# Eight transformer layers on one core: q turned by VectorE and DRAM, two heads per column group, ternary tails in one product

## The chip, the cores and the metric

The program runs on one NeuronCore of a Trainium2 chip. The metric is the device time of one execution in microseconds (us). A core has TensorE (matrix products and transposes through its array, PE in the profile), VectorE (DVE), ScalarE (ACT), GpSimd (POOL), SyncE (SP, which here only issues DMAs) and 16 DMA engines. Each engine runs its own instruction list in order and meets the others at semaphores. TensorE writes to PSUM, which the kernel uses as eight banks of 128 partitions x 512 float32 columns.

## The reference, cut to what matters

The input x is 16 tiles of 128 rows x 256 columns; the context has 128 rows x 128 columns per tile. Eight layers follow each other, each of the form x = x + layer(layernorm(x)): attention and feed-forward in turn. Three attention layers and one feed-forward are touched:

```python
# first attention: 32 heads of 8, rotary positions on q and k
logits = jnp.einsum('bqhd,bkhd->bhqk', rope(x @ Wq), rope(k)) / sqrt(8)
out = einsum('bhqk,bkhd->bqhd', softmax(logits), v) @ Wout + bout    # one softmax per head
# small-head attention (third attention): 16 heads of 16, q and k normalised per head
#   two softmaxes per head: over the 112 main keys and over the last 16 keys
ctx = attn(q, k, v) + attn(q, k_dca, v_dca);  out = ctx @ Wo + bo
# ternary feed-forward: 682 hidden columns
h1 = x @ tern(w1).T; h3 = x @ tern(w3).T;  out = (silu(h1) * h3) @ tern(w2).T
# wide attention (fourth attention): 16 heads of 128
q = rmsnorm(x @ Wq, gq); k = rmsnorm(ctx @ Wk, gk)
out = (softmax(q @ k.T / sqrt(128)) @ v) @ Wo
```

(The excerpt is condensed; the shapes are those of the reference.) The other layers are a product-key feed-forward, a grouped attention with 16 heads of 128, a routed mixture of experts and a feed-forward with block-quantised operands.

## The kernel before, in words

The work is cut into stages 0 to 7, one for each layer (the mixture of experts has the sub-stages 3, 8 and 9), and each stage into steps. A step is done for each tile b and, in some, for parts c. `STEPS` lists for each stage its steps, their parts and the engines that have a share in them (T, V, A, G, S for TensorE, VectorE, ScalarE, GpSimd, SyncE); `ONCE` lists work done once per stage. `ORDER` holds one long string for each engine: each letter is the next part of one step, so the order of every engine's whole program is written out, and stages overlap where the strings mix them. `BANKS` gives the PSUM banks of each step; a helper `room` makes TensorE wait until the bank's last content was taken, `full` and `freed` give the semaphore and count at which a bank has been filled or emptied. A wait stands ahead of the instruction that needs it, and everything behind it on that engine waits too.

**Stage 0** (`small_heads` with s = 0). Per tile: layer norm (`lnA`, `lnB`), transposes of the normalised tile (`xT`), q and k in one bank (`qk`, L943 to L948), rotation (`rope`, L1821 to L1823 on VectorE, L2520 on GpSimd), a split of q and k into float16 high parts and rests (`split`: ScalarE L1433, GpSimd's two copies L2525 and L2526, VectorE's two subtractions L1867 and L1868, all at once), 16 float16 transposes (`tqk`, L971), score products for the row maximum (`mx`, L995), eight maxima (`mxr`, L1887), transposes of q with its maximum (`tq2`, L1024), score products again with keys in rows (`st`, L995), eight exponentials (`ex`, L1465), and value products (`pv`, L1042): for each part c four products of one head each, 32 output partitions by 128 columns. Eight parts fill two banks, `oa` and `ob`, that is 1024 columns, of which 9 rows in 32 are used (8 values and the sum of the exponentials). Two copies (`ot`, L1472), eight transposes back (`tb`, L1052), two divisions (`norm`, L1907 and L1911), the output product (`oT`, `out`).

**Stage 4** (`small_heads` with s = 4) is alike with 16 heads of 16. Its two kinds of score products are interleaved: a step `ms` (L1016 and L1012) holds maximum products of tile b in one pair of banks (3 and 4) and softmax products of tile b - 1 in another (5 and 6); `sl` does the last tile's. Four matmuls in turn use four groups of 32 array rows. k's scale and bias are applied by VectorE while it copies the transposes (L1878, L1879); v is copied by VectorE in two masked forms with its bias (`vp`, L1899). The inverse roots of 32 variances per row are GpSimd's (`nb`, L2533).

**Stage 5** (`ternary`). w1 and w3 as signs in bfloat16; the 682 hidden columns are five tiles of 128 and one of 42 for each of w1 and w3. Step `h` (L1274) with c = 1 does the last full tile and the 42-column tile of each, six products per tile of columns (three bfloat16 parts of x, two halves of the inner dimension).

**Stage 6** (`wide_heads`). 16 tiles x 4 parts = 64 steps, four heads of 128 in each. q (L1301, L1302) goes to bank 0; ScalarE copies it (L1644) and squares it (L1647); TensorE transposes it head by head (`tq`, L1314) and ScalarE copies the transposes with a scale (L1658). k (L1308) is squared (L1652), normalised (L2313 on VectorE, L2564 and L2566 on GpSimd, L2324), turned in blocks of 32x32 by VectorE (L2333), written to DRAM by a DMA from GpSimd's queue (L2555) and read back by four DMAs from SyncE's queue (L866), which completes the 128x128 transpose. Score products (L1323), row maximum (L2347), exponentials with their sums (L1673), the reciprocal and the multiplication of P (`pn`, L2356 and L2358 on VectorE), P's own turn (L2341, L2560, L866), the product with the context (`pv`, L1329), a copy (L1664) and the output product (`wo`, L1337).

**Stage 7** (`quantized`) runs in part beside stage 6: products L1359, L1360 and L1376; on VectorE a chain of operations over 1024 columns (L2368 to L2391).

## Time and profile before

| | us |
|---|---|
| timed runs | 2088.37, 2077.08, 2078.17 |
| median | 2078.17 |
| profiled execution | 2088.02 |
| its span | 2085.8 |
| mean granted TensorE clock | 0.989 of full |
| busy: TensorE / VectorE / ScalarE / GpSimd | 1997.6 / 1713.2 / 1274.0 / 667.7 |

The span runs from the first to the last instruction. Busy time is the union of the instructions of an engine; waiting, semaphores and the issuing of DMAs are not in it, save that GpSimd's DMA instructions count as its own. A matmul's end is modelled, so a group of pipelined matmuls looks some 0.2 us longer than the time until the next group may start. One float32 matmul of the program appears as two MATMUL rows (a transpose as one).

### The profile page before, as it was taken

What the parts mean: (1) busy time and instruction counts of PE and PEld (TensorE: products, weight loads), DVE (VectorE), ACT (ScalarE), POOL (GpSimd) and SP (SyncE); (2) the same over time, 40 slices, a digit from 0 to 9 for tenths busy, and PEclk for the clock granted to TensorE, in tenths of its full rate; (3) what the DMA queues carried; (4) which work ended last, traced back from release to release, by engine and by line L of the source; (5) the groups of instructions that cost most, each with busy time, mean ns of one, the idle gap of its engine ahead of it and who ended that gap; (6) DMA issues with size and microseconds to landing.
All of it is one profiled execution on the core that took longest, in us unless ns stands there. A gap on an engine that the chain in (4) does not pass through costs nothing.

```text
span 2085.8 us, 46042 instructions
## 1 busy us (share of the span) xinstructions
PE 1997.6 (96%) x16294; PEld 1564.6 (75%) x16294; DVE 1713.2 (82%) x4655; ACT 1274.0 (61%) x3214; POOL 667.7 (32%) x1000
## 2 busy tenths in 40 slices
PE   5999899999999999998998889999999999999998
PEld 3666799999988888877997667887665666656665
DVE  7887899999689997766447789896887998888877
ACT  3778988798944554544653444634766666567552
POOL 6321020000012232222128776111665345434420
PEclk8999999999999999999999899999999999999999
DMA  9400300000045443433220010023544233333320
GB/s 336 144 3 2 124 6 2 2 2 2 12 151 168 137 151 104 142 102 89 89 65 26 29 62 2 2 87 122 166 150 133 91 112 114 127 105 107 122 81 25
DMA packets 181515, 182.28 MB, mean 87 GB/s; under 512 B 20678, under 2 KB 160088, under 8 KB 180264
## 3 DMA queue, kind: packets, MB, share of 16 engines
q1 hardware_dynamic: 160168, 112.49, 17.5%
q0 software_dynamic: 21120, 66.87, 8.8%
q8 instruction: 130, 2.13, 0.4%
q14 instruction: 97, 0.79, 0.1%
HBM read 99.06 MB, written 80.22 MB: 86 GB/s over the span
## 4 chain that ended last, share of the span: by engine, by line
PE 53%; DVE 29%; issue 7%; ACT 4%; POOL 4%; DMA 3%; SPq 1%; another core or an unknown queue 0%; DVEq 0%; ACTq 0%; POOLq 0%
PE pb L1141 4%; PE pb L1164 3%; PE pb L1274 3%; PE pb L1337 2%; PE pb L1042 2%; PE pb L1149 2%; PE pb L1376 2%; PE pb L1359 2%; PE pb L1222 2%; PE pb L1360 2%; PE pb L1156 2%; PE pb L1283 2%; PE pb L995 2%; PE pb L1213 2%; PE pb L1329 1%
## 5 line engine op out<-in xcount | busy, mean ns | idle before, releaser
L2472 POOL TENSOR_SCALAR sm<-sm 128x1 f32<-128x1 f32 x128 | 33.7, 263 | 455.9 <-DVE sm L1745 454.9
L1508 ACT ACTIVATE areaB<-i128h,workB 128x128 f16<-128x128 f16 x512 | 156.2, 392 | 0.1
L1465 ACT ACTIVATE areaA<-pb 128x512 f32<-128x512 f32 x192 | 106.8, 600 | 61.6 <-PE pb L1012 35.2
L1535 ACT ACTIVATE workA<-workA 128x128 f32<-128x128 f32 x256 | 99.4, 390 | 60.8 <-DVE workA L2059 55.5
L1673 ACT ACTIVATE workA<-pb,workA 128x128 f32<-128x128 f32 x256 | 113.9, 460 | 30.9 <-DVE workA L2351 30.3
L1097 PE MATMUL pb<-areaB 128*128 128x128 f32 x1024 | 126.7, 280 | 3.1 <-ACT workB L1498 2.9
L1141 PE MATMUL pb<-xT,areaA 128*128 128x128 f32 x1024 | 124.2, 276 | 0.0
L1097 PEld LDWEIGHTS pb<-areaB 128*128 128x128 f32 x1024 | 119.8, 194 | 5.6 <-ACT workB L1498 3.3
L1141 PEld LDWEIGHTS pb<-xT,areaA 128*128 128x128 f32 x1024 | 120.0, 192 | 4.5 <-issue 4.0
L1164 PE MATMUL pb<-areaA,workA 128*128 128x256 f32 x512 | 121.6, 382 | 0.9 <-ACT workA L1542 0.9
L1337 PE MATMUL pb<-areaA,workA 128*128 128x256 f32 x512 | 120.7, 380 | 0.0
L2541 POOL DMA_DIRECT2D turn<-workA x64 | 37.1, 580 | 245.3 <-DVE workA L2072 244.8
L1113 PE MATMUL pb<-areaB,workB 128*128 128x256 f32 x512 | 113.7, 380 | 1.1 <-DVE workB L2036 1.1
L1337 PEld LDWEIGHTS pb<-areaA,workA 128*128 128x128 f32 x512 | 95.0, 190 | 25.3 <-issue 12.9
L1164 PEld LDWEIGHTS pb<-areaA,workA 128*128 128x128 f32 x512 | 93.8, 190 | 21.6 <-issue 8.5
L1113 PEld LDWEIGHTS pb<-areaB,workB 128*128 128x128 f32 x512 | 96.0, 190 | 13.9 <-DVE workB L2036 1.3
L1887 DVE TENSOR_REDUCE workA<-pb 128x4 f16<-128x512 f32 x128 | 83.4, 689 | 13.9 <-PE pb L995 13.5
L1042 PE MATMUL pb<-areaA,workA 128*32 128x128 f32 (+1 forms) x1536 | 86.4, 285 | 5.3 <-ACT areaA L1465 4.3
L2533 POOL TENSOR_TENSOR areaA<-areaA,neghalf 128x32 f32<-128x32 f32 x16 | 87.6, 5475 | 1.3
L1323 PEld LDWEIGHTS pb<-workA 128*128 128x128 f32 x512 | 65.1, 191 | 21.7 <-issue 18.6
L2474 POOL TENSOR_TENSOR sm<-sm,neghalf 128x1 f32<-128x1 f32 x128 | 76.7, 599 | 10.7
L1664 ACT COPY workA<-pb 128x512 f32<-128x512 f32 x64 | 37.8, 590 | 66.5 <-PE pb L1329 66.0
(426 smaller groups left out, 5872.0 us busy)
## 6 DMA issues: line engine op xcount, KB each, us to landing
turn<-workA POOLq DMA_DIRECT2D x64, 256.0 KB
workA<-turn SPq DMA_DIRECT2D x256, 64.0 KB
turn3k<-areaA POOLq DMA_DIRECT2D x64, 256.0 KB, 2.7
workA<-turn3k SPq DMA_DIRECT2D x256, 64.0 KB, 2.0
turn3p<-areaA POOLq DMA_DIRECT2D x64, 256.0 KB, 2.7
rows_in<-areaB SPq DMA_DIRECT2D x7, 2048.0 KB, 16.5
areaA<-turn3p SPq DMA_DIRECT2D x168, 64.0 KB, 2.0
workA<-turn3p SPq DMA_DIRECT2D x88, 64.0 KB, 2.0
```

What stands on the lines that cost most here:

```text
L1042: m = eng.matmul(p[r, k * 128:(k + 1) * 128], vt[:, h, :], P[:, j * 128:(j + 1) * 128], start=True, stop=True)
L1097: m = eng.matmul(p[:, e * 128:(e + 1) * 128], w.ed[:, k, (4 * c + e) * 128:(4 * c + e + 1) * 128], xT[:, k, :], start=(k == 0), stop=(k == 1))
L1113: m = eng.matmul(p[:, 0:256], G[:, e, :], w.eu[:, e, :], start=(e == 0), stop=(e == 15))
L1141: m = eng.matmul(p[:, h * 128:(h + 1) * 128], w.wq[:, 4 * c + h, k], xT[:, k, :], start=(k == 0), stop=(k == 1))
L1164: m = eng.matmul(p[:, 0:256], u.OT[i][:, h], w.wo[:, 4 * c + h], start=(c == 0 and h == 0), stop=(c == 3 and h == 3))
L1337: m = eng.matmul(p[:, 0:256], u.OT[i][:, h], w.wo[:, 4 * c + h], start=(c == 0 and h == 0), stop=(c == 3 and h == 3))
L1465: eng.activation(u.P[n % RP], bank(*held)[:, :], ACT.Exp, scale=1.0 / math.sqrt(hd)).then_inc(freed(*held)[0], 1)
L1508: m = eng.activation(u.far[:, g], i128h[:, :], ACT.Square, bias=u.at[b % 2][:, 8 * c + g:8 * c + g + 1])
L1535: m = eng.activation(u.P[i][:, h], u.P[i][:, h], ACT.Exp, accum_out=u.den[i][:, h:h + 1], bias=u.nm[i][:, h:h + 1])
L1673: m = eng.activation(u.P[i][:, h], p[:, h * 128:(h + 1) * 128], ACT.Exp, accum_out=u.den[i][:, h:h + 1], bias=u.nb[i][:, h:h + 1], scale=u ...
L1887: eng.tensor_reduce(o[:, :, 24:25], p, AX.X, ALU.max, negate=True).then_inc(freed(s, tag, b, c // 2)[0], 1)
L2533: eng.tensor_tensor(va, va, neghalf[:, 0:32], ALU.pow).then_inc(S["l2_rs"], 1)
```

## The change

What it does:

- Stage 6: VectorE turns q out of PSUM in blocks of 32x32, GpSimd's queue writes it to DRAM (`turn3q`), SyncE's queue reads it back in four DMAs, ScalarE scales it from SBUF into the place that the scores product reads. TensorE's step `tq` and ScalarE's plain copy of q are gone. q's products use banks 0 and 3 in turn. The multiplication of P by the reciprocal moves from VectorE to GpSimd.
- Stage 0: the second half of the heads is laid 16 columns later in its 32-column group of the value operand, so that heads of parts c and c + 4 accumulate in one group of 32 partitions; one bank `o` of 512 columns replaces `oa` and `ob`; one copy, four transposes, one division. The rows of Wout are permuted on the way in. The two subtractions of the split move from VectorE to GpSimd, behind its copies.
- Stage 4: `mx` and `st` are separate steps of 16 matmuls over four row groups; both use the banks 3 to 6. k's scale and bias and v's two masked forms move from VectorE to ScalarE; v's bias is added at the output transposes' copy (two ScalarE passes in place of one copy).
- Stage 5: the 42 last columns of w1 and the 42 of w3 (rolled to the front of their block) stand 64 columns apart and are done by one product of 106 columns.
- Stage 3: TensorE's rank product waits for the position of the tile before (`m_pos`).
- The strings of `ORDER` are new for all engines.

```diff
# TensorE, stage 0: value products, back transposes
-                    k = (c - c0) * (E // 32) + E * j // 128
+                    k = c % 4 if s == 0 else (c - c0) * 2 + j // 2
                     m = eng.matmul(p[r, k * 128:(k + 1) * 128], vt[:, h, :], P[:, j * 128:(j + 1) * 128],
-                                       start=True, stop=True)
+                                       start=(s == 4 or c == 0), stop=(s == 4 or c == 7))
+                elif step == "tb" and s == 0:
+                    t.wait_ge(*freed(0, "o", b))
+                    p = room(0, "r", b)
+                    for k in range(4):
+                        m = eng.transpose(p[:, k * 128:(k + 1) * 128], u.OTs[b % 2][:, k * 128:(k + 1) * 128], ident)
...
# GpSimd, stage 0: split
                     eng.tensor_copy(qp[:, 0, :, 16:24], qp[:, 0, :, 0:8])
                     eng.tensor_copy(qp[:, 1, :, 8:16], qp[:, 1, :, 0:8])
+                    eng.tensor_tensor(qp[:, 0, :, 8:16], y4[:, 0], qp[:, 0, :, 0:8], ALU.subtract)
+                    eng.tensor_tensor(qp[:, 1, :, 16:24], y4[:, 1], qp[:, 1, :, 0:8], ALU.subtract).then_inc(S["l0_split"], 1)
...
# stages 0 and 4: score products (a step of stage 4 is now all four row groups)
+                    rows = range(2 * (c % 2), 2 * (c % 2) + 2) if s == 0 else range(4)
+                    tags = [step + "ab"[i % 2] if s == 0 else f"{step}{i}" for i in rows]
+                    p = [room(s, tag, b, c) for tag in tags]
-    (4, "ms"): lambda b, c: (("mxa", 3), ("mxb", 4)) + ((("sta", 5), ("stb", 6)) if b else ()),
+    (4, "mx"): lambda b, c: (("mx0", 3), ("mx1", 4), ("mx2", 5), ("mx3", 6)),
+    (4, "st"): lambda b, c: (("st0", 3), ("st1", 4), ("st2", 5), ("st3", 6)),
...
# ScalarE, stage 4: k's scale and bias, v's two forms
+                            eng.activation(dst[:, :, 0:112], src[:, :, 0:112], ACT.Identity, scale=w4.nwc[:, 1:2], bias=w4.nwc[:, 4:5])
+                            eng.activation(dst[:, :, 112:128], src[:, :, 112:128], ACT.Identity, scale=w4.nwc[:, 2:3],
+                                           bias=w4.nwc[:, 5:6]).then_inc(freed(4, "tk", b)[0], 1)
+                    for k in range(2):
+                        m = eng.activation(u.vt[b % RV][:, :, 17 * k:17 * k + 16], src, ACT.Copy, scale=side[k])
...
# TensorE, stage 3
+                    if b > 0:
+                        t.wait_ge(S["m_pos"], b)
...
# TensorE, stage 5
+                        tiles = [(128 * m_, at + 128 * (4 * c + m_), 128) for m_ in range(4 if c == 0 else 1)]
+                        if c == 1 and tag == "h3":
+                            tiles.append((128, 640, 106))
...
# stage 6: TensorE, VectorE, GpSimd, SyncE, ScalarE
-    (6, "q"): lambda b, c: (("q", 0),),
+    (6, "q"): lambda b, c: (("q", (0, 3)[c % 2]),),
-                elif step == "tq":
-                    t.wait_ge(S["l3_qn"], nth(b, c, 4))
-                    p = room(6, "tq", b, c)
-                    for h in range(4):
-                        m = eng.transpose(p[:, h * 128:(h + 1) * 128], u.qn[i][:, h * 128:(h + 1) * 128], ident)
+                    eng.transpose(u.Dq[n % 2].rearrange("p (j h w) -> p j h w", j=4, h=4),
+                                  bank(6, "q", b, c)[:, :].rearrange("p (h j w) -> p j h w", h=4, j=4)).then_inc(S["l3_qt"], 1)
+                    eng.dma_start(turn3q[n % 4], u6.Dq[n % 2].rearrange("p (j w) -> p j w", j=4)).then_inc(S[f"l3_qw{n % 2}"], 16)
+                    turned_in(turn3q[n % 4], u6.qr[n % 2], S[f"l3_qr{n % 4}"])
+                    eng.activation(u.qT[i].rearrange("p h (i w) -> p h i w", i=4),
+                                   u.qr[i].rearrange("p (i h w) -> p h i w", i=4, h=4), ACT.Copy, scale=gp[:, 0:1]).then_inc(S["l3_qg"], 1)
-                    eng.tensor_tensor(u.P[i], u.P[i], bc(u.rec[i], 2, [128, 4, 128]), ALU.mult).then_inc(S["l3_pn"], 1)
+                elif step == "pn":
+                    g.wait_ge(S["l3_rec"], nth(b, c, 4))
+                    P, rec = u6.P[c % 2], u6.rec[c % 2]
+                    eng.tensor_tensor(P, P, bc(rec, 2, [128, 4, 128]), ALU.mult).then_inc(S["l3_pn"], 1)
```

## Rows read from the trace of the kernel before

**Rows 1.** The page, busy time of each engine and the chain that ended last.

```profile
PE 1997.6 (96%) x16294; PEld 1564.6 (75%) x16294; DVE 1713.2 (82%) x4655; ACT 1274.0 (61%) x3214; POOL 667.7 (32%) x1000
...
PE 53%; DVE 29%; issue 7%; ACT 4%; POOL 4%; DMA 3%; SPq 1%; another core or an unknown queue 0%; DVEq 0%; ACTq 0%; POOLq 0%
```

**Rows 2.** Windows: from:to, length, busy PE, PEld, DVE, ACT, POOL (count), clock, DMA, GB/s.

```profile
50.00:200.00 150.00, 147.51 (x2418) 101.86 (x2411) 127.13 (x272) 116.94 (x218) 36.92 (x69) 1.00 0.17 56
...
1110.00:1310.00 200.00, 175.55 (x1963) 138.41 (x1961) 166.11 (x463) 88.67 (x163) 145.75 (x121) 0.94 0.09 28
...
1450.00:1600.00 150.00, 145.45 (x633) 93.63 (x634) 120.37 (x258) 107.61 (x291) 89.69 (x147) 1.00 0.50 160
...
1450.00:2086.00 636.00, 617.62 (x2542) 397.61 (x2542) 531.32 (x1008) 389.53 (x975) 271.26 (x436) 1.00 0.35 113
```

**Rows 3.** TensorE by shape: busy us, mean ns, idle; last: duration min/median/max, first, last.

```profile
L1314 PE MATMUL pb<-cst,workA 128*128 128x128 f32 x256 | 38.5, 273 | 1.5 <-ACT workA L1658 1.0 <-ACT xT L1422 0.4
...
L1274 PE MATMUL pb<-workB,areaB 128*128 128x128 bf16 x960 | 60.4, 219 | 0.0
...
L1274 PE MATMUL pb<-workB,areaB 128*42 128x128 bf16 x192 | 16.4, 221 | 0.0
...
L1191 PE MATMUL pb<-workB,cst x16: 166/169/180, 626.2 to 959.7; 128*128 128x8 f16 x16
```

**Rows 4.** TensorE in order of time: start us, us, line.

```profile
118.75 0.61 PE L1052 MATMUL pb<-cst,areaA 128*128 128x128 f32 x4
...
119.28 0.40 PE L995 MATMUL pb<-workA 32*128 32x128 f16 x8
...
1710.11 0.60 PE L1314 MATMUL pb<-cst,workA 128*128 128x128 f32 x4
...
1710.55 1.02 PE L1329 MATMUL pb<-areaA,workA 128*128 128x512 f32 x2
```

**Rows 5.** VectorE, groups by shape.

```profile
L2333 DVE STREAM_TRANSPOSE areaA<-workA 128x512 f32<-128x512 f32 x64 | 45.1, 704 | 11.5 <-DMA turn3k<-areaA 9.1 <-ACT areaA L1637 1.9
...
L2358 DVE TENSOR_TENSOR workA<-workA 128x512 f32<-128x512 f32 x64 | 44.5, 696 | 2.2
...
L1889 DVE TENSOR_REDUCE workA<-pb 128x4 f32<-128x448 f32 x64 | 39.5, 617 | 10.2 <-PE pb L1016 6.3 <-remote 3.8
...
L1899 DVE SCALAR_TENSOR_TENSOR workA<-pb,cst,areaA 128x256 f32<-128x256 f32 x32 | 13.9, 475 | 0.2 <-PE pb L962 0.2
...
L1878 DVE TENSOR_SCALAR workA<-pb,areaA 128x448 f32<-128x448 f32 x16 | 11.8, 737 | 2.6 <-PE pb L979 2.6
...
L1879 DVE TENSOR_SCALAR workA<-pb,areaA 128x64 f32<-128x64 f32 x16 | 5.3, 334 | 0.0
```

**Rows 6.** ScalarE, groups by shape.

```profile
L1465 ACT ACTIVATE areaA<-pb 128x512 f32<-128x512 f32 x192 | 106.8, 600 | 61.6 <-PE pb L1012 35.2
...
L1658 ACT ACTIVATE workA<-pb,gp 128x512 f32<-128x512 f32 x64 | 44.6, 696 | 22.1 <-PE pb L1314 22.1
```

**Rows 7.** GpSimd, groups by shape.

```profile
L2515 POOL TENSOR_TENSOR x<-x,areaA 128x256 f32<-128x256 f32 x32 | 24.0, 758 | 15.1 <-DVE xn L1755 15.1
...
L2520 POOL TENSOR_TENSOR workA<-workA 128x512 f32<-128x512 f32 x16 | 20.6, 1286 | 9.0 <-DVE workA L1868 5.4 <-DVE workA L1823 3.7
```

**Rows 8.** Lines L1867 and L2566: duration ns min/median/max.

```profile
L1867 DVE TENSOR_TENSOR workA<-workA x16: 415/421/1484, 23.3 to 189.9; 128x256 f16<-128x256 f32 x16
...
L2566 POOL TENSOR_TENSOR workA<-workA,neghalf x64: 1006/1032/2027, 1431.7 to 1997.8; 128x4 f32<-128x4 f32 x64
```

**Rows 9.** DMA: issue on GpSimd, KB and us to landing, SyncE's issue of four.

```profile
L2555 POOL DMA_DIRECT2D turn3k<-areaA x64 | 38.7, 605 | 56.4 <-DVE areaA L2333 55.6 <-issue 0.4
...
turn3k<-areaA POOLq DMA_DIRECT2D x64, 256.0 KB, 2.7
...
areaA<-turn3p SPq DMA_DIRECT2D x168, 64.0 KB, 2.0
...
1699.85 1.77 SPq L866 DMA_DIRECT2D areaA<-turn3p  x4
```

More of the change, by code:

```diff
@@ L557, in program @@
         w4.mu = carve(32)
-        w4.bvs = [carve(256).rearrange("p (h e) -> p h e", e=16) for _ in range(2)]
+        w4.bvT = carve(4).rearrange("p (j k) -> p j k", j=2)
+        w4.bsum = carve(2)
         carve = carver(area[0], 4096)
@@ L609, in program @@
         u6.kn = carve(512)
-        u6.qn = [carve(512) for _ in range(2)]
+        u6.Dq = [carve(512) for _ in range(2)]
         u6.qT = [carve(512).rearrange("p (h n) -> p h n", n=128) for _ in range(2)]
+        u6.qr = [work[1][:, 8704 + 512 * k:9216 + 512 * k] for k in range(2)]
         u6.kT = [carve(512) for _ in range(2)]
@@ L980, in small_heads @@
                         m.then_inc(full(s, tag, b)[0], 1)
-                elif step in ("mx", "st") and s == 0:
+                elif step in ("mx", "st"):
                     if step == "mx":
@@ L1444, in small_heads @@
                     if b >= RQ and step == "tqk":
-                        a.wait_ge(*full(*scores(s, 1, b - RQ, ng // 2 - 1)))
+                        a.wait_ge(*full(*last_square(s, "st", b - RQ)))
                     if s == 0:
@@ L1476, in small_heads @@
                         a.wait_ge(*full(s, "out", b - 2))
-                    eng.copy(u.OT[b % 2], bank(s, "oT", b)[:, 0:256].rearrange("p (k n) -> p k n", k=2)
-                             ).then_inc(freed(s, "oT", b)[0], 1)
+                    src = bank(s, "oT", b)[:, 0:256].rearrange("p (k n) -> p k n", k=2)
+                    if s == 0:
+                        eng.copy(u.OT[b % 2], src).then_inc(freed(s, "oT", b)[0], 1)
+                    else:
+                        for k in range(2):
+                            m = eng.activation(u.OT[b % 2][:, k], src[:, k], ACT.Identity, bias=w4.bsum[:, k:k + 1])
+                        m.then_inc(freed(s, "oT", b)[0], 1)
             def peer(step, b, c):
```

395 lines of the change are left out of this document (197 added, 198 removed), and 23 rows, old and new, of tables (ONCE, STEPS, TAKEN).

## The prediction

> **What bounds the kernel now.** I read the busy shares first, then the chain of waits, the windows by stage, and the groups by shape of the engines that the change touches. TensorE is busy 96% of the span and carries 53% of the chain that ended last; VectorE, the second, is busy 82% and carries 29% [rows 1]. The windows show where each bound sits [rows 2]. In the first attention (50 to 200 us) TensorE is busy 147.5 of 150 us. Where the fifth layer's small-head attention runs (1110 to 1310 us) it is busy 175.6 of 200: there 24.4 us are idle, VectorE is busy 166.1, and the granted clock of 0.94 shows that part of the stretch ran at 1.2 GHz instead of 2.4. In the wide attention and the last feed-forward (1450 to 2086 us) TensorE is busy 617.6 of 636, VectorE 531.3, ScalarE 389.5, GpSimd 271.3. So an instruction taken off TensorE shortens stage 0 and stages 6 and 7 nearly at its price, if nothing comes late in its place; in stage 4 VectorE and the order of hand-overs decide as well.
>
> A group's busy time is too dear a price for a matmul, since it holds the pipelined tail of the last one. The timeline gives the rate [rows 4]: four transposes are shown as 0.60 us, but the next product starts 1710.55 - 1710.11 = 0.44 us after the first of them. In the first attention the same four occupy 119.28 - 118.75 = 0.53 us.
>
> **The change, part by part.**
>
> Wide attention (stage 6, 64 steps). Four TensorE transposes go from every step: 64 x 0.44 = 28.2 us off the engine; the group's 38.5 us is the upper bound [rows 3, 4]. Their work moves:
> - VectorE turns q out of PSUM. The same shape from SBUF takes 704 ns [rows 5], so 45.1 us come. Nothing shows this turn with a PSUM source; The ends I keep are 0.60, the shortest ScalarE pass over 512 columns [rows 6], and 0.84 us, VectorE's PSUM read of 448 columns in 737 ns scaled to 512 [rows 5]; I take the SBUF row, as the same operation. In return the multiplication of P leaves VectorE: 64 x 696 ns = 44.5 us. VectorE stays at about 531 us, against 636 - 28 = 608 us of stage: 87%.
> - ScalarE drops the plain copy of q (about the 0.60 us of a 512-column pass [rows 6]) and keeps the scaling copy of 696 ns [rows 6], now from SBUF. It is busy 390 of 636 us, so this gives nothing.
> - GpSimd gets the multiplication and one more DMA issue. Its nearest row is the 128x512 addition, 1286 ns [rows 7]; the issue of an equal block is 605 ns [rows 9]. So 64 x 1.89 = 121 us come, and GpSimd stands at 271 + 121 = 392 of 608 us. But the opening of the stage is denser: in 1450 to 1600 it is busy 89.7 us with 19 steps [rows 2], and 19 x 1.89 = 36 makes 126 of 150. The next LayerNorm statistics, both reciprocal roots and three DMA issues queue behind each multiplication.
> - SyncE issues four more reads per step, 1.77 us for four [rows 9]: with q it issues three sets, 5.3 us, in a step of 608 / 64 = 9.5 us.
> - q's road to the scores product is now 0.70 (turn) + 0.61 (issue) + 2.7 (landing) + 1.77 + 2.0 (four reads, landing) + 0.70 (scaling) = 8.5 us, where it was a copy, four transposes and a copy, 1.8 us. In the new order of TensorE's queue I counted the work that stands between the q product and the scores product of the same step, at 0.43 us for 512 columns: 8.0 us at the least, 14.8 in the median. Without queueing on the way one step is short, by 0.5 us; with 1 us of queueing six are, by 5.9 us together; with 3.5 us eleven, by 25. k's road is longer still, but k is issued earlier (median 25 us). The P road grows by 1.29 - 0.70 = 0.6 us, and the order gives it 20 us in the median where it gave 17. I take 6 us of new idle time in all; the ends are 0 and 64 x 1.3 = 83 us (the rival below).
> Net: 28.2 - 6 = 22 us.
>
> First attention (stage 0, 16 tiles). Two heads now share 32 output partitions, so the output is 512 columns and not 1024; the number of value products is the same. Four of the eight back transposes go: 16 x 0.53 = 8.6 us; upper bound 16 x 0.61 = 9.8 us [rows 4]. ScalarE loses one copy and VectorE one division of 16 heads per tile: both hidden. The two subtractions of the split move from VectorE to GpSimd: 2 x 758 ns by the 128x256 addition [rows 7], 24 us in a stage where GpSimd is busy 36.9 of 150 us. They were done beside the copies on GpSimd and now come after them, so TensorE's transposes of q and k start about 1 us later in each tile's chain; the next tile's work covers it, and without that cover it costs 16 us. I take 8.6 us.
>
> Ternary layer (stage 5). The two products of 42 columns per part become one of 106: 12 instructions to 6 per tile, 96 in all. The streamed operand is 128 columns either way. At the main form's 60.4 / 960 = 63 ns this is 6.0 us; at the narrow form's 16.4 / 192 = 85 ns, 8.2 [rows 3]. I take 6.
>
> Small-head attention (stage 4). The score products of max and softmax no longer run interleaved in two pairs of banks; both now use the same four banks, in turn. Their number and their rotation over four row groups stay. VectorE sheds k's scaling (737 + 334 ns) and v's two masked forms (2 x 475): 2.0 us per tile, 32 us in all, to ScalarE, which was busy 88.7 of the 200 us [rows 2, 5]; the bias of the output, now two passes instead of one copy, is ScalarE's too. That lets TensorE come nearer to its own work; all 24.4 us of idle time is the most it can give. Against it stands the hand-over of banks. After the max products four pairs of reductions must run, 4 x 617 ns and four over the other 64 columns at 334 ns or less, 2.5 to 3.8 us [rows 5], and after the softmax products four exponentials, 2.4 us [rows 6], before the other kind may start. The new order puts 1.3 to 5 us of other TensorE work between them; adding up where it is less than needed I get some 10 us of sure idle time, in place of the stalls that were there. I take a gain of 4 us, between +24 and -20.
>
> The new wait of the rank product on the previous tile's position costs nothing: the 16 rank products are spread over 626 to 960 us [rows 3], some 20 us apart, and only the few small VectorE operations of one tile stand between rank and position.
>
> **Sum.** 22 + 8.6 + 6 + 4 = 41 us. The profiled execution took 2088.0 us (span 2085.8), so it would take 2047. The three timed runs have a median of 2078.2, 9.9 below the profiled one; with the same saving the median comes to 2037 us.
>
> **A rule weighed.** Rows first [rows 8]: VectorE's subtraction with two SBUF operands takes 421 ns in the median and 1484 at worst, and GpSimd's power of four elements 1032 and 2027. So the two engines do hold each other up, by about one instruction of the other.
> The Trainium skill (SBUF — State Buffer, Who interferes with whom) says that VectorE and GpSimd share one pair of SBUF ports under an exclusive lock, and that whoever comes second waits for the whole instruction. It speaks against moving a 128x512 multiplication to GpSimd. [...] The excess of 1.06 us in the rows agrees with a wait for one instruction.
>
> **Rivals.**
> 1. GpSimd's multiplication holds VectorE. Worked from rows: if each of the 64 blocked VectorE for its full 1.29 us, VectorE would have 531 + 82 = 613 us and bind the stage, which then saves nothing: gain 8.6 + 6 + 4 = 19, time 2060. For it: the worst cases above. Against it: most VectorE work there reads PSUM or one operand, and one such multiplication leaves VectorE itself.
> 2. The bank turn of stage 4 costs more: its idle time grows by 20 instead of shrinking by 4: 2078 - 41 + 24 = 2061. For it: the short gaps in the new order, each needing a prompt VectorE, and VectorE busy 83% there. Against it: its 32 us less of work.
> 3. Slower: q's road through DRAM sets the pace. GpSimd takes its turns in order, and in the opening of stage 6 it is at 84% or more; if q comes late by 1.3 us in each step, 83 us are lost and the 6 counted are not: 2078 - 41 - 6 + 83 = 2114. It decides from 41 / 64 = 0.64 us of mean lateness per step beyond what I counted. Against it: 14.8 us of cover in the median for a road of 8.5.
> 4. Better: TensorE keeps every instruction's group price and stage 4's idle time goes: 38.5 + 9.8 + 8.2 + 24.4 = 81, time 1997.
> That the work is not removed can be excluded: the transposes are gone from the program.
>
> **How the numbers follow.** Forecast 0.6, rivals 0.08, 0.12, 0.09, 0.11. The likeliest case itself spans 2022 to 2052 (new idle time in stage 6 of 0 to 15 us, stage 4 between +10 and -5). To leave out no more than 2 in 10 the range takes in rivals 1 and 2 and half of the way to 4: 2012 to 2066. What a measurement of this kernel can tell from no change is about 0.5%, 10 us: faster means under 2067.8, slower over 2088.6. Faster gets the forecast, rival 4 and two thirds of 1 and 2, 0.84, less 0.02 for what I did not see; same 0.08; slower 0.10 (rival 3 and a little).
>
> **What would show it.** Right: no transposes from the q step; TensorE busy about 40 us less and its share still 94% or more; the wide stretch about 22 us shorter; in it few waits of the scores product on ScalarE's scaled q; a turn of q near 0.70 us on VectorE and a multiplication near 1.29 on GpSimd; idle time of TensorE in the small-head stretch about 20 us. Wrong: TensorE waiting for the scaled q or for the reads of q in most steps (rival 3); VectorE over 95% there with lengthened instructions (1); first score products of stage 4 waiting for reductions or exponentials with more than 30 us in sum (2).

## The result and the profile after

The changed kernel takes 2076.02 us (median of 20 runs, 2072.09 to 2083.57); the kernel before took 2080.51 beside it (20 runs, 2075.52 to 2088.37). The ratio is 0.9979, 95% interval 0.9970 to 0.9987: 4.5 us faster. The interval leaves out 1, so the kernel is a little faster, but by less than half of the 0.5% that the prediction took as the least that can be told, and far from the 2037 us that were forecast. The profiled execution took 2075.69 us, span 2073.7.

The page after, answering to [rows 1]: 416 TensorE instructions and 44 us of its busy time are gone, and the span is 12 us shorter, not 40 (and 7 of the 12 were a lateness of that one execution of before, as shown below). Its share falls to 94%. In the chain that ended last, TensorE falls from 53% to 40%, and SyncE's queue, the DMAs and GpSimd rise from 8 to 16%.

```profile
PE 1953.9 (94%) x15878; PEld 1517.6 (73%) x15878; DVE 1683.4 (81%) x4527; ACT 1261.0 (61%) x3209; POOL 782.4 (38%) x1160
...
PE 40%; DVE 33%; issue 8%; POOL 7%; DMA 5%; SPq 4%; ACT 4%; DVEq 0%; POOLq 0%; ACTq 0%
```

The windows, with the columns of [rows 2]. In the opening of the wide attention TensorE was idle 4.6 of 150 us before and is idle 9.4 after, GpSimd is busy 118 us and not 90, and the DMA share is 0.73 instead of 0.50.

```profile
50.00:200.00 150.00, 144.55 (x2393) 97.76 (x2390) 114.31 (x222) 112.47 (x207) 49.32 (x95) 1.00 0.17 55
...
1450.00:1600.00 150.00, 140.60 (x543) 87.45 (x543) 125.91 (x264) 96.44 (x274) 118.34 (x185) 0.98 0.73 226
1450.00:2074.00 624.00, 583.37 (x2222) 362.23 (x2221) 525.56 (x981) 351.42 (x891) 351.02 (x538) 0.99 0.51 161
```

The new operations cost about what was estimated. These are the groups of the changed kernel for VectorE's turn of q, GpSimd's multiplication, its third issue and ScalarE's scaling, answering to [rows 5, 6, 7, 9]: 698 ns against 704 taken, 1067 against 1286, 592 against 605, and 726 against 696. On the right of each row stands how long the engine was idle before these instructions and what ended it: ScalarE stood 68.5 us for the reads of q (`turn3q`).

```profile
L2326 DVE STREAM_TRANSPOSE workA<-pb 128x512 f32<-128x512 f32 x64 | 44.6, 698 | 6.0 <-PE pb L1313 5.2 <-DMA turn3q<-workA 0.7
...
L2587 POOL TENSOR_TENSOR workA<-workA 128x512 f32<-128x512 f32 x64 | 68.3, 1067 | 19.6 <-DVE workA L2373 18.9
...
L2573 POOL DMA_DIRECT2D turn3q<-workA x64 | 37.9, 592 | 62.1 <-DVE workA L2326 61.6
...
L1688 ACT ACTIVATE workA<-workB,gp 128x512 f32<-128x512 f32 x64 | 46.5, 726 | 69.0 <-DMA workB<-turn3q 68.5 <-PE pb L1328 0.4
```

The waits of TensorE and of its weight loads in stages 6 and 7 (engine, line, what it waited for: us in total, times, longest). L1334 is the product with P, L1328 the scores. L1334 stood 30.7 us for turn3p in sum, L1328 17.6 us for ScalarE's scaled q.

```profile
PEld pb L1334 <- DMA areaA<-turn3p: 12.9, 11, 2.7
PEld pb L1328 <- ACT workA L1688: 12.0, 12, 2.1
PEld pb L1334 <- DMA workA<-turn3p: 7.6, 8, 2.9
...
PE pb L1328 <- ACT workA L1688: 5.6, 6, 1.3
PE pb L1334 <- DMA areaA<-turn3p: 5.5, 9, 1.8
PE pb L1334 <- DMA workA<-turn3p: 4.7, 3, 2.6
```

The same waits of the kernel before, whose product with P is L1329: 8.2 us.

```profile
PEld pb L1329 <- DMA workA<-turn3p: 3.5, 5, 1.0
...
PEld pb L1329 <- DMA areaA<-turn3p: 1.9, 3, 0.7
...
PE pb L1329 <- DMA workA<-turn3p: 1.6, 3, 0.8
PE pb L1329 <- DMA areaA<-turn3p: 1.2, 3, 0.5
```

### The profile page after: what moved, and what is told of

The parts are those of the page before. It is cut to its first block, busy times and chain, and to the rows that moved or that the text cites. A ratio compares the mean times of both kernels' runs of the same rounds, so it can differ in the third digit from the quotient of the medians.

```text
span 2073.7 us, 45659 instructions
## 1 busy us (share of the span) xinstructions
PE 1953.9 (94%) x15878; PEld 1517.6 (73%) x15878; DVE 1683.4 (81%) x4527; ACT 1261.0 (61%) x3209; POOL 782.4 (38%) x1160
## 4 chain that ended last, share of the span: by engine, by line
PE 40%; DVE 33%; issue 8%; POOL 7%; DMA 5%; SPq 4%; ACT 4%; DVEq 0%; POOLq 0%; ACTq 0%
PE pb L1148 3%; PE pb L1171 3%; SPq L877 3%; PE pb L1040 3%; PE pb L1013 3%; PE pb L1156 2%; PE pb L1231 2%; PE pb L1163 2%; PE pb L1222 2%; DVE workB L1952 1%; PE pb L1120 1%; DVE workB L2042 1%; PE pb L1104 1%; POOL workA L2593 1%; DVE workB L2033 1%
## 5 line engine op out<-in xcount | busy, mean ns | idle before, releaser
L1104 PE MATMUL pb<-areaB 128*128 128x128 f32 x1024 | 124.6, 278 | 0.0
L1013 PE MATMUL pb<-workA 32*128 32x128 f16 (+2 forms) x2048 | 82.0, 252 | 9.7 <-DVE workA L1904 4.4
L1328 PEld LDWEIGHTS pb<-workA 128*128 128x128 f32 x512 | 65.2, 192 | 33.6 <-issue 20.9
L1688 ACT ACTIVATE workA<-workB,gp 128x512 f32<-128x512 f32 x64 | 46.5, 726 | 69.0 <-DMA workB<-turn3q 68.5
L1013 PEld LDWEIGHTS pb<-workA 32*128 32x128 f16 (+2 forms) x2048 | 58.9, 140 | 39.2 <-issue 24.9
```

The lines of the kernel that those rows point to most:

```text
L1013: m = eng.matmul(p[k][:, j * 128:(j + 1) * 128], one, two, start=True, stop=True)
L1104: m = eng.matmul(p[:, e * 128:(e + 1) * 128], w.ed[:, k, (4 * c + e) * 128:(4 * c + e + 1) * 128], xT[:, k, :], start=(k == 0), stop=(k == 1))
```

## The experiments

Whole runs of this kernel scatter by some 5 us, and chips differ: the median of before was 2080.5 to 2087.5. So the ratio is given, and beside it a measure that scatters less, called the stretch from here on: from the first q product of stage 6 to the last output product of stage 7, by the first and last starts of those lines. For the changed kernel it is 2070.7 - 1426.4 = 644.3 us:

```profile
L1312 PE MATMUL pb<-areaA,xT x128: 592/592/1061, 1426.4 to 1994.7; 128*128 128x512 f32 x128
```

```profile
L1381 PE MATMUL pb<-areaB,workB x256: 379/379/455, 1617.2 to 2070.7; 128*128 128x256 f32 x128
```

A second trace of the changed kernel gives 644.4. The kernel before was traced again too, since its first trace came from an execution of 2088.0 us, 7.5 over its median:

> The kernel before, unchanged, for a second trace of it: the first came from an execution of 2088.0 us where its median was 2080.5. If the 8 us lie in its stages 0 to 5, the last product of stage 5 stands here at about 1430 us instead of 1439, and stages 6 and 7 (first q to last output product) at 636 us in both. If they lie in stages 6 and 7, that stretch is here near 629 us, and then the changed kernel's 644 is 15 us longer, not 8.

This execution took 2081.15 us; the stretch is 2076.0 - 1440.3 = 635.7, and it was 636.0 in the first trace. So the 7 us lay ahead of stage 6 (first q at 1440.3 here, 1446.9 there).

```profile
L1301 PE MATMUL pb<-areaA,xT x128: 592/592/697, 1440.3 to 1992.2; 128*128 128x512 f32 x128
```

```profile
L1376 PE MATMUL pb<-areaB,workB x256: 379/379/454, 1631.0 to 2076.0; 128*128 128x256 f32 x128
```

The wide attention and what follows it thus became 8.5 us longer, where 22 us shorter was forecast: 30 us are missing. The windows over the stretch, with the columns of [rows 2], for the kernel before (second trace), the changed kernel, and the changed kernel without any road for q (e4 below):

```profile
1440.30:2076.00 635.70, 619.61 (x2552) 399.52 (x2551) 531.09 (x1007) 391.15 (x978) 271.47 (x436) 1.00 0.36 115
...
1426.40:2070.70 644.30, 603.13 (x2301) 373.93 (x2300) 538.15 (x1003) 365.45 (x917) 364.58 (x562) 0.99 0.52 165
...
1432.30:2048.20 615.90, 593.91 (x2300) 373.13 (x2300) 500.77 (x939) 393.02 (x981) 327.88 (x498) 1.00 0.36 118
```

TensorE is idle 16.1 us before and 41.2 us after: 25 us of new idle time, where 6 were taken. And its busy time falls by 16.5 us, not by the 25.7 of e4, though it does the same products: in three stretches of 20 us (from 1446, 1506 and 1906 us) the changed kernel was granted a clock of 0.91, and some products took up to 1061 ns where the median is 592.

The table has all runs of these two stages, with what each does in a few words. A ratio has 1.8 to 6 us of uncertainty. The stretch stands on one trace for each run, save where two are given. Traces of one kernel differ by 0.1 to 0.3 us in it, but e9 and e11, which differ only in the bytes of a write whose data nobody uses, by 4.4. Differences of a few us between two rows are to be read with that in mind.

| kernel | stages 6 and 7, us | ratio to before [95%] |
|---|---|---|
| before | 636.0, 635.7 | 1 |
| changed | 644.3, 644.4 | 0.9979 [0.9970, 0.9987], again 0.9984 [0.9974, 0.9994] |
| e1: P divided on VectorE | 650.1 | 0.9989 [0.9973, 1.0006] |
| e3: both parts undone | 637.0, 636.7 | 0.9955 [0.9937, 0.9973], 0.9950 [0.9930, 0.9970] |
| e2: old order, division alone on GpSimd | 712.1 | 1.0301 [1.0273, 1.0329] |
| e12: the same, placed otherwise | 706.7 | 1.0280 [1.0267, 1.0294] |
| e4: q without any road | 615.9 | 0.9838 [0.9813, 0.9864] |
| e5: + VectorE's turn | 624.3 | 0.9884 [0.9864, 0.9904] |
| e9: + GpSimd's write | 632.3 | 0.9935 [0.9915, 0.9955] |
| e11: e9 with a small write | 636.7 | 0.9930 [0.9915, 0.9944] |
| e10: + four small reads | 635.4 | 0.9932 [0.9911, 0.9954] |
| e6: + reads in full | 643.8 | 0.9968 [0.9953, 0.9983] |
| e7: changed, ScalarE off q's road | 642.3 | 0.9967 [0.9954, 0.9980] |
| e8: changed, one read for four | 641.4 | 0.9958 [0.9944, 0.9971] |
| e16: changed, q's write by SyncE | 674.2 | 1.0127 [1.0099, 1.0155] |

**Each part undone.**

```
- eng.reciprocal(u.rec[i], u.den[i]).then_inc(S["l3_rec"], 1)      # e1; GpSimd's "pn" empty
+ eng.reciprocal(u.rec[i], u.den[i]).then_inc(*v.mark()); v.settle()
+ eng.tensor_tensor(u.P[i], u.P[i], bc(u.rec[i], ...), ALU.mult).then_inc(S["l3_pn"], 1)
```

> The changed kernel, but the division of P in the wide attention is VectorE's again (reciprocal, then the multiplication straight behind it); q still goes through DRAM. In the changed kernel a step's P reaches its turn 4.4 us after the reciprocal ends, before 1.45 us. Theory A (P's road is late, because GpSimd takes its instructions in order and P's multiplication stands behind other work and waits there): most of the 36 us that stages 6 and 7 lost comes back, 2050 to 2058 us, and the waits of the pv product on turn3p fall from 31 us of idle time to under 12. Theory B (q's own road makes the scores late: ScalarE waits 68 us in all for q's reads and the score products 18 us for ScalarE): little changes, 2070 to 2078, and the score waits stay. Theory D (SyncE's queue and the DMA traffic of twelve issues a step delay every road alike): 2066 to 2076, waits for both stay at half or more. VectorE as the bound (64 x 0.7 = 45 us more work on it) would give 2080 or more.

Nothing comes back: the stretch gets 6 us longer, the ratio moves by 0.001, which its interval can't tell from none. By the timeline's means over 64 steps, P's way from the end of the reciprocal to the start of its turn is 4.4 us in the changed kernel (1.45 before) and 4.5 in e1: the new order has the turn later anyway. So e1 does not shorten P's road and can't clear it; it shows that in this order the division on GpSimd costs nothing, and by the stretch of one trace gains 6 us.

e3 takes the code and the queue orders of the kernel before for stages 6 and 7 and leaves the rest changed.

> Stages 6 and 7 wholly as in the kernel before (q transposed on TensorE, P divided on VectorE, the old order), stages 0 to 5 as changed. The trace has the last product of stage 5 26.5 us earlier and the first q of stage 6 20.5 us earlier than before, and stages 6 and 7 took 639 us before against 648 us after. If the parts add up, 2080.5 less 20 to 26 = 2054 to 2060 us. If the gain of the stages ahead is swallowed at the boundary (the weights of stage 6 or 7 arrive late, or the clock falls), 2066 to 2076.

> The run with both parts of the wide attention undone, timed again beside the changed kernel on one chip. It was at 0.9955 of the kernel before, with stages 6 and 7 at 637 us (before 636, changed 644). Expected 0.993 to 0.997, and 3 to 8 us below the changed kernel.

> The changed kernel, unchanged, on the same chip as the run with both parts undone: 0.997 to 0.999 of the kernel before; stages 6 and 7 again near 644 us.

The marks of the second run of e3, 2071.9 - 1435.2 = 636.7:

```profile
L1470 PE MATMUL pb<-areaA,xT x128: 592/592/697, 1435.2 to 1987.5; 128*128 128x512 f32 x128
```

```profile
L1545 PE MATMUL pb<-areaB,workB x256: 379/379/454, 1627.5 to 2071.9; 128*128 128x256 f32 x128
```

The stretch is as before, to 1 us. Timed beside each other on one chip, e3 ran in 2076.7 us (median of 7), the changed kernel in 2083.2 (11), the kernel before in 2087.1: the change to stages 0 to 5 alone is the best version that leaves nothing out, 10.4 us under before. (20 to 26 were expected in the first run; they came from the first trace of before, with its 7 us of lateness.) So the wide attention's edit costs 6.5 us by the times and 7.5 by the stretch.

**The division alone.** e2 has e3's code and orders, with P's multiplication moved to GpSimd and VectorE's turn of P one instruction later; e12 has the turn further back and GpSimd's order taken from VectorE's.

> Stages 6 and 7 in the order and with the q transposes on TensorE of the kernel before; of the change to the wide attention only the division of P on GpSimd is kept, with VectorE's turn of P one instruction later in its order. All other stages as changed. Starting point is 2080.5 - 24.5 (what the changed stages 0 to 5 gained in the trace) = 2056. Theory A (the multiplication on GpSimd costs lateness whatever q does): 2066 to 2080. Theory B or D (it is q's road that costs): 2050 to 2058.

> Stages 0 to 5 as changed; in stages 6 and 7 q is transposed on TensorE in the order of the kernel before, and the division of P is on GpSimd as in the run that came to 1.030, but placed otherwise: VectorE's turn of P stands three instructions behind the reciprocal, not one, and GpSimd takes its instructions in the order in which VectorE releases them. If that run's 64 us came from VectorE standing at its turn for the product (69 us of idle time there), this one is at 0.990 to 1.000, and if the division on GpSimd frees VectorE to some use, below the run with both undone (0.9955). If it came from the longer road of P itself, it stays above 1.010.

By the stretch they are 75 and 70 us slower than e3; e12 lies where a longer road of P was to put it. In e2 VectorE stood at its turn for the product:

```profile
DVE areaA L2523 <- POOL workA L2749: 71.7, 41, 3.2
```

In e12 that is mostly gone (12.7 us), but now the product with P waits on TensorE. The rows of its weight loads and its matmuls:

```profile
PEld pb L1503 <- DMA areaA<-turn3p: 29.3, 15, 6.0
PEld pb L1503 <- DMA workA<-turn3p: 14.7, 7, 7.8
```

```profile
PE pb L1503 <- DMA areaA<-turn3p: 24.4, 12, 5.2
PE pb L1503 <- DMA workA<-turn3p: 12.6, 5, 7.6
```

I read this as: the old order of TensorE has no room for a later P, the changed kernel's has. The same division on GpSimd costs 70 us in one order and nothing, or less than nothing, in another. (The two orders differ in more than P's place, so how much a still better placing would save stays open.)

**What q's road costs, piece by piece.** e4 lets ScalarE copy q and nothing else happen to it:

> The changed kernel with the transposition of q left out altogether: ScalarE copies q from the bank and scales the copy, nothing goes to VectorE, GpSimd or DRAM for it (the scores are those of an untransposed q). It shows what TensorE's 64 x 0.44 us are worth when q has no road. Theory A (P's road on GpSimd holds): no better than the changed kernel less a little, 2062 to 2074, pv still waits for turn3p. Theory B or D (q's road, or the traffic that it adds): 2036 to 2050, near the 2037 forecast. In between: both.

The gain is there: 615.9 us, 28.4 less than the changed kernel and 21 less than e3.

```profile
L1308 PE MATMUL pb<-areaA,xT x128: 592/592/697, 1432.3 to 1971.2; 128*128 128x512 f32 x128
```

```profile
L1377 PE MATMUL pb<-areaB,workB x256: 379/379/454, 1614.2 to 2048.2; 128*128 128x256 f32 x128
```

Theory A falls with it: GpSimd divides here as well, and P is nearly as late (4.2 us from reciprocal to turn, against 4.4). But the 21 us are not the transposes alone: without the division and without q's turn VectorE has 30 us less to do than before (500.8 against 531.1). With q's turn in, VectorE's work is back at 537.1 and 12.5 us of the gain over e3 are left (e5). Then the pieces of the road were put back one at a time.

```
  eng.activation(u.qT[i]...,                                      # e5, e6, e9 to e11: what ScalarE scales
-     u.qr[i]..., ACT.Copy, scale=gp[:, 0:1])                     #   what came back from DRAM
+     u.cx[:, 0:4]..., ACT.Copy, scale=gp[:, 0:1])                #   a resident block of the same size
- a.wait_ge(S[f"l3_qr{n % 4}"], 64 * (n // 4 + 1))
+ a.wait_ge(S["l3_qt"], n + 1)
  # e5: no write, no reads.  e9: write.  e11: write of rows 0 to 15.  e10: write, reads of 4 rows.  e6: all
```

> The changed kernel with VectorE's turn of q left in place, but no write to DRAM and no reads for q: ScalarE waits for the turn and then scales a resident block of the same size instead of the q that came back (q's values are left out of the scores). Against the kernel before, the changed kernel is at 0.998 and q with no road at all (no turn, no DMA) at 0.984. If VectorE's 64 turns of 0.70 us are what costs (VectorE is the engine busiest beside TensorE), this run is near 0.996 to 1.000. If it is the road through DRAM or its DMAs, it stays near 0.984 to 0.987.

```profile
L1308 PE MATMUL pb<-areaA,xT x128: 592/592/697, 1431.4 to 1977.2; 128*128 128x512 f32 x128
```

```profile
L1377 PE MATMUL pb<-areaB,workB x256: 379/379/454, 1614.8 to 2055.7; 128*128 128x256 f32 x128
```

> As the run with the turn alone, and now with the write to DRAM and the four reads of each step issued as in the changed kernel, but no computing engine waits for them: only SyncE, GpSimd and the DMA queues carry them (q's values are again left out of the scores). If the queues and the traffic are the cost (SyncE with twelve reads a step, GpSimd with three writes a step, DMA share 0.52 for 0.35, which delays K's and P's reads too), this run is at 0.994 to 0.999. If the cost is the latency of q's own road, for which ScalarE waits in its order (68 us of idle time there), it stays near the run with the turn alone, within 0.003 of it.

```profile
L1312 PE MATMUL pb<-areaA,xT x128: 592/592/1061, 1427.3 to 1993.4; 128*128 128x512 f32 x128
```

```profile
L1381 PE MATMUL pb<-areaB,workB x256: 379/379/454, 1619.2 to 2071.1; 128*128 128x256 f32 x128
```

> As the run with VectorE's turn alone (0.988 of the kernel before), plus GpSimd's issue of q's write and the write itself (64 x 0.59 us on GpSimd, 16.8 MB); SyncE reads nothing back. The same with the reads and no one waiting was 0.997. If GpSimd's third issue a step delays the writes of K and P, this run is at 0.994 to 0.997. If it is SyncE's four further reads a step or their bytes, it stays at 0.988 to 0.991.

```profile
L1308 PE MATMUL pb<-areaA,xT x128: 592/592/697, 1424.1 to 1979.5; 128*128 128x512 f32 x128
```

```profile
L1377 PE MATMUL pb<-areaB,workB x256: 379/379/454, 1609.5 to 2056.4; 128*128 128x256 f32 x128
```

> As the run with the write alone (0.9935; its stages 6 and 7 took 632 us in the trace, against 624 with the turn alone), but the write carries 16 of 128 rows, 32 KB for 256 KB; GpSimd issues it as often. If GpSimd's issuing in its order is the cost (64 x 0.59 us between its pow and multiplication instructions), stages 6 and 7 stay at 631 to 634 us and the ratio at 0.992 to 0.995. If it is the bytes of the write, 624 to 627 us and 0.988 to 0.990.

> As the run with all of q's DMAs and no one waiting (0.997), but each of the four reads of a step brings 4 rows x 4 pieces instead of 32 x 4, so 8 KB instead of 64 KB: SyncE issues as often, the queues carry an eighth. If the issuing on SyncE is what delays the reads of K and P, it stays at 0.994 to 0.998. If it is the bytes in the DMA engines, it falls to the time of the write alone, 0.988 to 0.992.

The pieces by the stretch:

- The turn on VectorE 8.4 us. Its ratio of 0.9884 lies between the two expectations, nearer to the second: it is a third of the loss, not all and not nothing. It is a net price, since ScalarE's plain copy of q goes in the same step.
- The write 8.0, and with an eighth of its bytes not less (636.7). So it is GpSimd's issue and not the bytes; VectorE, which may not turn q into a buffer before its last write has landed, waited 0.2 us for that in all of e9.
- SyncE's four issues a step at most 3.1, perhaps nothing: 635.4 lies between the two runs with a write alone, 632.3 and 636.7.
- The other seven eighths of the read bytes 8.4 (7.1 if e11 is taken for e9).
- ScalarE's wait for them 0.5.

Together 28.4. Each step stands on one trace. The ratios give the same ladder, 9.6, 10.6, -0.6, 7.5 and 2 to 3 us, with 4 to 7 us of uncertainty on each difference. What the issue of 0.59 us delays is only in part seen: from e5 to e9 and e11 P's division starts 1.97 and 1.92 us after its reciprocal where it was 1.68, while the time from a turn's end to its issue's end hardly moves (P 1.29 to 1.33 and 1.36, K 1.35 to 1.46 and 1.41). That k's reciprocal roots on GpSimd come later too is how I read it; no run separates the two.

No computing engine takes q's data in e6, yet it has nearly all of the loss, and it shows as waits for P. In e5, matmuls only:

```profile
PE pb L1330 <- DMA workA<-turn3p: 2.4, 4, 0.7
PE pb L1330 <- DMA areaA<-turn3p: 1.5, 2, 1.1
```

and in e6:

```profile
PE pb L1334 <- DMA areaA<-turn3p: 10.5, 11, 1.8
PE pb L1334 <- DMA workA<-turn3p: 4.1, 4, 1.5
```

K's reads landed in 2.0 us in e5 and in 2.3 us in e6, the writes in 2.6 to 2.7 and 2.7 to 2.8. With the weight loads the waits for turn3p grew by 26 us, from 15.1 to 41.4; the stretch grew by 19.5. From P's issue to the copy of its product the mean grew from 10.2 to 10.7 us, but some 0.3 of that is the slower pace itself (19.5 us over 64 steps) and no cause of it. The Trainium skill (Trainium Kernel Development and Optimization, Key Constraints) says that DMAs of all issuing queues run on the same 16 engines, and that a further queue saves issue time only. The first half agrees with e6 and e10: q's bytes cost 8.4 us and K's reads land later, while SyncE's issues cost 3 at most. The second half no run here tests, since q's DMAs use queues that were there.

**Two ways to ease it, and one to move it.**

> The changed kernel with ScalarE taken off q's road: its scaling of q (64 x about 0.6 us) is left out, and TensorE's score product waits for the reads itself and takes q as it lies (the interchange of blocks and the weight by dimension are left out). If ScalarE, standing in its order at q's reads, holds the exponentials and copies behind it, most of the 28 us comes back: 0.984 to 0.989. If the latency simply reaches TensorE, the wait moves to the score product and the time is 0.993 to 1.000. If queues and traffic delay K and P too, likewise 0.993 or more, with the pv waits on turn3p still there.

> The changed kernel with q read back by one DMA of 256 KB in whole rows instead of four of 64 KB in pieces of 128 bytes (the exchange of the 32-row blocks is left out, so the scores are of a q in the wrong order). SyncE issues nine reads a step instead of twelve. If SyncE's issuing or the small pieces are the cost: 0.986 to 0.991, with the waits for turn3q and turn3p both smaller. If it is the latency of a road through DRAM as such: 0.995 to 0.999.

> The changed kernel with q's write to DRAM issued by SyncE instead of GpSimd, one set of K reads earlier in SyncE's order than the reads of q. The ladder of runs put 8 us on GpSimd's third issue a step and nothing on SyncE's further issues. If that holds, the changed kernel gains 6 to 10 us, 0.993 to 0.996, with stages 6 and 7 near 636 us. If SyncE stands at the write for VectorE's turn and holds the reads of K and P behind it, nothing is gained or time is lost: 0.998 to 1.005.

e7 takes away the 68.5 us that ScalarE stood idle, the largest of its waits, and its 46.5 us of scaling with them, and 2 us come of it. e8 gains 3 us and lands at the low end of "latency as such" (the pieces of the four reads are 512 bytes, not 128 as the expectation has it). e16 loses 30 us: SyncE, in its order, stood 48 us at the new write for VectorE's turn (the last row), and K's and P's reads queued behind; the products with P and their weight loads then waited 55 us for turn3p, against 30.7. The first two rows are not new: SyncE stood 95.6 and 76.5 us for those landings in the changed kernel.

```profile
SPq L884 <- DMA turn3p<-areaA: 79.6, 26, 9.1
SPq L884 <- DMA turn3q<-workA: 63.7, 33, 7.2
SPq L909 <- DVE workA L2339: 48.4, 14, 9.9
```

**The other stages.** Both runs start from e3.

```
- for k in range(4):                       # e13, stage 0: back transposes twice
+ for k in (0, 1, 2, 3, 0, 1, 2, 3):
+     tiles.append((256, 640, 106))        # e13, stage 5: the ternary tail product twice
+ if c: eng.tensor_reduce(idle[...], w.bqk..., AX.X, ALU.add)   # e14, stage 4, VectorE, three per tile
```

> The run with both parts of the wide attention undone (0.995 of the kernel before), and on TensorE two things done twice that the change saves once: the four back transposes of each tile of the first attention (the forecast prices them at 16 x 0.53 = 8.5 us) and the product of 106 ternary columns (96 instructions, 6.0 us). If the prices hold: 14.5 us more, 1.002; stage 1's last gather product 8 us later than 554 us, and from the first to the last product of the ternary layer 6 us more than 123.5. If the engine had slack there that takes them up, less: 0.995 to 0.998.

> The run with both parts of the wide attention undone, and in the small-head attention (stage 4) VectorE does three further 128x512 reductions of a constant in each tile, 3 x 0.68 = 2.0 us, as much as it shed to ScalarE there (k's scaling and the two masked forms of v). The forecast gave stage 4 a gain of 4 us; the traces show 11 for stages 4 and 5 together. If the gain came from VectorE's 32 us less, this run loses about what was gained above the ternary layer's 6: 5 to 10 us, and 0.998 to 1.000. If it came from the order and the banks, it stays within 2 us, 0.994 to 0.997.

e13 is at 0.9966 [0.9949, 0.9984], 2 to 4 us above e3 and not 14.5. Stage 1's last gather product comes at 557.2 us, 3.0 later than the mean of fifteen traces of kernels with stages 0 to 5 as changed (all but e13, e14 and e16; 552.8 to 556.1), where 8.5 us were added ahead of it. From the first to the last product of the ternary layer it takes 124.6 us, 1.2 more than e3, for 6.0 added. TensorE's slack takes up most of what is added. (Its own trace, of an execution 4.4 us over the median, has the first q product at 1445.1, 10 us later than the latest of the fifteen; most of that arises between 557 and 1305 us, in stages that this edit leaves alone. So single marks in the middle of the kernel scatter by several us.) e14 is at 1.0103 [1.0080, 1.0126]: 28 us over e3 by the medians and 32 by the ratios, for 48 reductions of 674 ns, 32 us: nearly their full price. Four windows of the small-head attention in e14 and their sum, with the columns of [rows 2]:

```profile
1125.00:1175.00 50.00, 40.17 (x444) 31.99 (x446) 38.09 (x102) 26.32 (x50) 38.95 (x36) 0.86 0.09 28
1175.00:1225.00 50.00, 44.18 (x512) 35.27 (x509) 36.35 (x104) 29.60 (x61) 37.09 (x27) 0.93 0.08 23
1225.00:1275.00 50.00, 42.05 (x418) 33.82 (x418) 47.46 (x123) 24.66 (x52) 37.49 (x35) 0.88 0.17 54
1275.00:1320.00 45.00, 40.41 (x502) 33.50 (x499) 38.32 (x106) 26.86 (x56) 24.11 (x20) 0.90 0.01 1
sum 195.00, PE 166.81 PEld 134.58 DVE 160.22 ACT 107.44 POOL 137.64; mean PE 41.70 PEld 33.65 DVE 40.05 ACT 26.86 POOL 34.41
```

The same of e3, first run:

```profile
1125.00:1175.00 50.00, 41.83 (x489) 33.59 (x489) 32.80 (x92) 30.56 (x58) 43.88 (x37) 0.93 0.10 28
1175.00:1225.00 50.00, 44.45 (x545) 35.50 (x547) 38.23 (x120) 29.20 (x62) 40.41 (x39) 1.00 0.12 33
1225.00:1275.00 50.00, 47.28 (x584) 39.01 (x586) 46.72 (x121) 32.27 (x66) 38.09 (x27) 1.00 0.13 44
1275.00:1320.00 45.00, 43.31 (x596) 36.37 (x593) 39.98 (x127) 34.08 (x70) 18.98 (x22) 1.00 0.01 2
sum 195.00, PE 176.87 PEld 144.47 DVE 157.73 ACT 126.11 POOL 141.36; mean PE 44.22 PEld 36.12 DVE 39.43 ACT 31.53 POOL 35.34
```

TensorE is idle 28 us there in place of 18. The granted clock stays at 0.86 to 0.93, so part of every one of these stretches ran at 1.2 GHz, where e3 has 2.4 from the second on. (The last stretch compares unlike work: the ternary layer starts at 1292.6 us in e3 and at 1317.8 in e14. In the first three the idle time is 23.6 us against 16.4.) How much of the 28 to 32 us is the lower clock was not separated.

## Why the prediction was wrong

**The step that failed** is "I take 6 us of new idle time in all" in the wide attention. TensorE got 25 us of it. The 28.2 us of transposes were priced about rightly: with them gone and no road in their place (e4), TensorE is busy 25.7 us less than before and idle 6 us more, which is the forecast, though e4 also has a VectorE with 30 us less to do. But q's road added 28.4 us, and the edit cost 7.5 us where I had it save 22. I had worked the road as a latency, 8.5 us against a cover of 14.8. That size was wrong too: from the end of q's product to the end of the scaling it takes 14.0 us in the mean, of which 2.3 pass before the turn begins. But the lateness of q is not what costs: e6 and e7 show that the wait for q is worth 0.5 to 2 us. What I left out is that the road takes time from three servers that K and P use too: VectorE (8.4 us), GpSimd's order (8.0) and the DMA engines (8.4). I had listed each load, 45, 121 and the issues, and had held each against its engine's mean share, 87%, 392 of 608 us, 5.3 of 9.5. In the changed kernel VectorE is busy 538 of 644 us, 84%, and yet q waits 2.3 us for it: a mean share doesn't say whether an engine is free at the moment it is asked.

**VectorE's balance.** That 45.1 us come and 44.5 go was right, and it was read as no cost. By one trace each, e5 prices the turn at 8.4 us and e1 the division at 6, a fifth and a seventh of their lengths, so the two about cancel, and the turn is a cost only against a kernel in which q has no road.

**P's road** "grows by 0.6 us": between reciprocal and turn it grew by 3.0 (4.4 for 1.45): GpSimd begins 1.9 us after the reciprocal, and VectorE turns 1.4 after the product. That was wrong and did little harm, since the new order covers it (in e4, with 4.2 us, the whole gain is there); in the old order the same move costs 70 us (e2, e12).

**Rival 1** fell: e1 says that without GpSimd's multiplication the kernel is no faster. It does lengthen single VectorE instructions: the 128x256 operation with two SBUF inputs of L2389 takes 550 ns in the mean in the changed kernel and 425 in e1, and the one of L2394 with a single SBUF input 373 against 300. **Rival 3** named the place, q's road, and the wrong mechanism: not q late but others late through q. **Rival 4** needed every price at its group's length, and the time is 79 us above it. **Rival 2** is below.

**Stages 0 to 5** were forecast at 8.6 + 6 + 4 = 18.6 us (16 x 0.53 is 8.5, a slip of 0.1) and gave about 10: e3 stands at 0.9955 and 0.9950, 9.4 and 10.4 us. At the first q product the fifteen traces have a mean of 1430.3 us (1424.1 to 1435.2) against 1440.3 in the second trace of before, which lies at its median: 10 us. (The first trace has 1446.9.) The parts can't be told so well, since the marks between scatter by some 4 us each way:

- Up to the last product of the expert layer the mean is 1117.4 against 1119.0 and 1124.6, so 2 to 7 us for the 8.6 of stage 0. e13 speaks for less than the price: adding that TensorE work again, with the ternary tail, costs 2 to 4 us and not 14.5. I had taken TensorE as the bound from 147.5 of 150 us busy, and a busy matmul is not one on the path.
- Stage 4, from there to the first ternary product, takes 175.2 us in the mean, 178.1 in the second trace of before (190.3 in the first, disturbed one): 3 us, where 4 were forecast. Rival 2 fell here. In the changed kernel the score products waited for the reductions that free their banks no more than this, and for exponentials not at all, so the 10 us of sure idle time at the bank turn do not show (8.3 us more of idle time ahead of them ended in no wait that the profile names):

```profile
PE pb L1013 <- DVE workA L1907: 1.9, 4, 0.9
```

- The ternary layer takes 130.0 us from its first to its last product in both traces of before and 123.4 in e3 (123.3 to 124.6 in the fifteen), 6 us less as forecast. But from there to the first q product it is 14.1 us in the mean and was 7.6, partly because the new order puts other products there, so how much of the 6 is left can't be told by these marks.

e14 shows that VectorE's time in stage 4 is worth nearly its full price when added. Why the 32 us taken from it brought so little is open: no run undid the banks or moved k's scaling back.

**The sum against the profiled execution.** The trace of 2088.0 us carried 7 us ahead of stage 6 that the median did not have. Taking the saving from the trace to the median, as I did, was right; but the window of stage 4, with 24.4 us idle and a clock of 0.94, came from the disturbed part: from 1120 to 1310 us the second trace has TensorE busy 170.3 of 190 us at a clock of 0.98, where the first has 166.6 at 0.94.

## What to carry to other kernels

Price a road through DRAM by what it takes from each shared server (the turning engine, the issuing engine's order, the DMA bytes), not by its latency against its cover: here the wait was worth 0.5 us of 28. Judge a wait by the run without it, not by its length: ScalarE's 68.5 us were worth 2, while the road that nobody waited for brought 26 us of waits for P on TensorE and its weight loads. And move an instruction to a queue only together with the order of whoever consumes it: the same division on GpSimd cost nothing in one order and took 70 us in another.

## What was not expected of the hardware

A write of 32 KB cost the kernel no less than one of 256 KB (stretch 636.7 and 632.3, ratio 0.9930 and 0.9935), and four further reads of 8 KB each at most 3 us, while those of 64 KB cost 8.4 us more. GpSimd multiplied 128x512 by a broadcast column in 1067 ns, where its addition of the same size took 1286 [rows 7]. VectorE's turn of 128x512 takes 698 ns from PSUM and 697 from SBUF.
